# A decoder kernel's first attention phase with another order of its stages, and constants loaded in another order

## The chip, the cores and the metric

The kernel runs as one program on one core of one Trainium2 chip. The metric is device time in microseconds (us) of one execution. All arithmetic is in 32-bit floats.

## The reference

Two decoder layers over x of 4 sequences x 1024 tokens x 256 numbers, with a context of 4 x 77 x 256. Each sublayer is followed by a layer norm of its sum with its input:

```python
x = _layernorm(x + _L0_attn_ref(x, ...))    # retention, 8 heads of 32: chunk by chunk,
#   attn = (q @ k.T) * D;  o = attn @ v + (q * decay_q) @ S
#   S = decay_s * S + (k * decay_k).T @ v
x = _layernorm(x + _L0_xattn_ref(x, ctx_1024, ctx_1024, W_out, b_out))  # softmax(q @ k.T) @ v, 16 heads of 16
x = _layernorm(x + _L0_ffn_ref(x, ...))     # 64 experts, the 8 best of each token, and 2 shared experts
x = _layernorm(x + _L1_attn_ref(x, ...))    # linear attention with a memory of 64 x 64
x = _layernorm(x + _L1_xattn_ref(x, ctx_1024, ...))
x = _layernorm(x + _L1_ffn_ref(x, ...))     # 8 experts, the 2 best of each token
```

## The kernel before

The program has four phases, one after the other on every engine: the first attention (both attention sublayers of layer 0, its router, and the sending of each token's row to the lists of its experts), the first expert phase, the second attention, the second expert phase. `attention_phase` is written once and called for both layers; `first` tells them apart.

An attention phase works in 8 steps of 128 positions of all four sequences (512 tokens). A step passes through some 50 stage parts. The order in which they are issued is a list written out by hand, `SEQUENCE0` for the first attention and `SEQUENCE1` for the second. An entry `(stage, ahead, part)` says: in round n do this part for step n - ahead. `steady` unrolls it over the rounds; entries whose step lies outside 0 to 7 are left out. Every engine walks the same list in program order and does its share of each entry, and semaphores couple the engines. So each engine is a queue: what waits holds up all that stands behind it on that engine.

The stages of the first attention are, in the order of a step's own dependences:

- Retention. `v` and `qk` (q and k) are products 128 x 128 by 512 tokens, moved out by ScalarE and VectorE. `kt` turns k. `ret` are the scores in 32 small products for two sequences, masked by VectorE with `causal`. `mix` forms the output in 64 small products. `up` advances the state. `wo` is the output product, with residual and norm sums on VectorE. `ln1` is the norm's scale on GpSimd and its use on ScalarE.
- Cross attention. `x1t` turns the rows. `mx` are 16 small products for the row maximum, `mt` turns the maxima, `sc` are the scores in 64 small products with the exponential on ScalarE. `pv` are 32 small products and a division on VectorE. `wout` is the output product, `ln2` its norm, `res` the residual with bias.
- Routing. `x2t` turns the rows, `rt` are the router logits, `top` chooses 8 of 64 experts (VectorE), `rank` counts places and yields `slots` (VectorE, L906 to L940). `cwt` and `b2` add the experts' second biases. `put` parts 0 to 7 are four indirect row transfers (scatters) each on GpSimd, from a `z2` buffer into `lists`. Some parts are preceded by a `rest`, a slow operation on four numbers a partition that spaces them out.

`wo`, `wout`, `v`, `qk`, `b2` and `rt` use the whole array in each product ("dense" below). `ret`, `mix`, `mx`, `sc`, `pv` and `up` use 32 rows or 32 columns of it, four side by side ("sparse" below).

PSUM has one wide tile of four banks, used in turn by `ret`, `mx` and `sc`, and four single banks used in rotation by all other product stages. A product waits until its bank was emptied.

SyncE (SP) issues the loads and stores in an order of its own: first `load(0)` (rows of step 0), `load_t(0)` (turned input of step 0), all constants (`loads`), step 1, the expert weights. Then in each of its iterations n it clears a part of `lists` (2 MB each, `lists<-zero`), stores x2s of step n-3, loads rows of step n+1, stores x2t of step n-2, loads turned input of step n+2, and stores the weights and places of step n-2. One semaphore, `consts`, counts all constants, and VectorE, TensorE and GpSimd wait for its full count. Then VectorE prepares `mask2`, `sel`, `scale_qk`, `state_mask`, `keys` and `vals` (L713 to L745, 24 operations counted by `ready`), and TensorE waits for all 24 before its first product (in the second attention, before the first product of step 0; the products of `keys` come ahead).

After the first attention, `with_units` puts 8 units of the shared experts between the last stages, and the expert phase begins with 20 more (L110 inward, L127 outward) before its first group of expert rows (`e_x<-lists`). The rows of step 7 are scattered at the start of the expert phase (L1544).

## Time and profile before

| | |
|---|---|
| time, median of 3 runs (lowest to highest) | 2013.31 us (2005.93 to 2014.84) |
| the profiled execution: its time, its span | 2014.15 us, 2012.2 us |
| busy share of the span: PE, PE weight load, DVE, ACT, POOL | 85%, 67%, 58%, 31%, 44% |
| mean granted clock of TensorE | 0.91 |
| chain that ended last, by engine | PE 60%, DVE 11%, POOL 8%, issue 7%, DMA 5% |
| last `rank` product of the first attention | 603.2 us |
| first expert rows of the first expert phase loaded | from 695.9 us |
| first product of the second attention | 1146.9 us |

PE is TensorE, PEld its weight load, DVE VectorE, ACT ScalarE, POOL GpSimd, SP SyncE. Times within the profile count from the start of the span. In a row of a timeline the columns are start, duration, engine, line of the kernel, operation, output and inputs, and in square brackets how long the engine sat idle before it and what released it. "issue" there means that it waited for nothing that the profile shows. The durations of pipelined products overlap, so a group of them is read from its start to the start of what follows. The granted clock is the share of TensorE's full clock.

### The profile page before, as it was taken

The numbers are of one execution on the slowest core, as the hardware profiler recorded it, in microseconds if no ns is written. First come the engines' busy times: TensorE is split into PE (matmuls) and PEld (weight loads), VectorE is DVE, ScalarE is ACT, GpSimd is POOL, SyncE is SP. The second block draws the span as 40 slices with busy tenths as digits, with TensorE's granted clock in tenths as the row PEclk, the third lists the DMA queues.
The fourth block names the chain that finished last, engine by engine and source line by source line (L and its number), as shares of the span: only waits on it lengthen the run. The fifth ranks groups of instructions, "written<-read, shape, count | busy, mean of one in ns | idle before, by whom it ended". The sixth has DMA issues, their size and how long they took to land.

```text
span 2012.2 us, 45539 instructions
## 1 busy us (share of the span) xinstructions
PE 1711.1 (85%) x17739; PEld 1349.4 (67%) x17739; DVE 1163.6 (58%) x3228; ACT 622.9 (31%) x957; POOL 895.1 (44%) x1000
## 2 busy tenths in 40 slices
PE   3788888888789899998998478899987499999994
PEld 2676666666656566665666345676656499999994
DVE  3576655755532176776656456787765345665554
ACT  0233222332221176544455123354432011111110
POOL 0006557556758201888888856333322201222223
PEclk9999978988679999999999678999887699999997
DMA  9415434545457899987999922113101512333332
GB/s 320 147 36 195 161 133 159 171 145 173 164 171 215 224 289 299 297 271 252 296 299 305 301 78 83 54 65 129 63 33 50 169 49 75 92 95 93 101 92 69
DMA packets 269634, 322.61 MB, mean 160 GB/s; under 512 B 25083, under 2 KB 245487, under 8 KB 268655
## 3 DMA queue, kind: packets, MB, share of 16 engines
q1 hardware_dynamic: 236399, 227.38, 35.7%
q0 software_dynamic: 33024, 92.32, 14.1%
q8 instruction: 144, 2.36, 0.5%
q14 instruction: 67, 0.55, 0.1%
HBM read 157.22 MB, written 162.40 MB: 159 GB/s over the span
## 4 chain that ended last, share of the span: by engine, by line
PE 60%; DVE 11%; POOL 8%; issue 7%; DMA 5%; ACT 3%; another core or an unknown queue 3%; SPq 1%; DVEq 1%; POOLq 0%; ACTq 0%
PE wide L2039 13%; PE d_yp L2051 6%; POOL big L1413 5%; PE wide L1171 4%; PE wide L1174 3%; PE wide L110 3%; PE wide L127 3%; PE bank L1191 3%; PE wide L1158 2%; PE bank L1184 2%; PE bank L1005 2%; PE bank L1148 2%; ACT pt L650 2%; PE bank L1077 2%
## 5 line engine op out<-in xcount | busy, mean ns | idle before, releaser
L1413 POOL DMA_INDIRECT big<-results,slots x256 | 268.4, 1048 | 207.0 <-DMA results<-e_y 127.3
L2039 PE MATMUL wide<-d_xt,d_ws 128*128 128x128 f32 x2272 | 278.4, 276 | 0.6 <-issue 0.6
L2039 PEld LDWEIGHTS wide<-d_xt,d_ws 128*128 128x128 f32 x2272 | 272.1, 193 | 4.5 <-issue 1.0
L588 POOL DMA_INDIRECT lists<-big,slots x160 | 159.1, 994 | 118.5 <-DVE slots L940 72.1
L650 ACT ACTIVATE pt<-wide 77x2048 f32<-77x2048 f32 x64 | 119.9, 1873 | 210.9 <-PE wide L1174 126.7
L1908 POOL DMA_INDIRECT d_picked<-results,slots x64 | 63.8, 997 | 181.5 <-DMA results<-d_y 168.2
L1939 ACT ACTIVATE d_gate<-wide 128x512 f32<-128x512 f32 x71 | 42.4, 597 | 324.6 <-PE wide L2039 320.0
L1428 DVE SCALAR_TENSOR_TENSOR big<-big,weights 128x256 f32<-128x256 f32 x256 | 108.9, 486 | 51.9 <-DMA big<-results,slots 33.9
L2051 PE MATMUL d_yp<-d_wd,d_h 128*128 x568 | 134.2, 379 | 0.0
L110 PE MATMUL wide<-shared_sx,shared_sw 128*128 128x512 f32 x256 | 127.0, 619 | 6.3 <-DMA shared_sx<-res_t 3.8
L127 PEld LDWEIGHTS wide<-shared_sw,shared_sh 128*128 128x128 f32 x512 | 99.8, 196 | 46.3 <-issue 29.9
L545 POOL TENSOR_TENSOR rs<-mv,eps 128x4 f32<-128x4 f32 x32 | 6.5, 202 | 277.1 <-DVE mv L699 276.9
L127 PE MATMUL wide<-shared_sw,shared_sh 128*128 128x256 f32 x512 | 124.9, 388 | 3.6 <-DVE big L1669 3.6
L158 POOL TENSOR_TENSOR rest_ones<-rest_ones 128x4 f32<-128x4 f32 x108 | 118.6, 1098 | 2.1
L2051 PEld LDWEIGHTS d_yp<-d_wd,d_h 128*128 128x128 f32 x568 | 102.6, 190 | 11.0
L1970 DVE COPY d_ws<-big 128x1024 f32 x142 | 92.5, 694 | 27.4 <-issue 26.4
L1559 ACT ACTIVATE e_xt<-e_xp 128x1024 f32<-128x1024 f32 x80 | 82.0, 1025 | 80.6 <-PE e_xp L1688 55.0
L1688 PE MATMUL e_xp<-e_ident,e_x 128*128 128x128 f32 x640 | 86.4, 279 | 21.8 <-DMA e_x<-lists 16.7
L1988 DVE TENSOR_TENSOR d_h<-d_gate,wide 128x512 f32<-128x512 f32 x71 | 48.7, 686 | 97.1 <-PE wide L2039 97.1
L1184 PE MATMUL bank<-pt,vals 77*32 77x128 f32 x2048 | 89.1, 311 | 15.0 <-issue 7.8
L1700 PE MATMUL wide<-e_xt,e_w1s 128*64 128x128 f32 x1280 | 90.2, 284 | 12.0 <-DVE e_w1s L1605 11.8
L1688 PEld LDWEIGHTS e_xp<-e_ident,e_x 128*128 128x128 f32 x640 | 72.1, 142 | 42.1 <-DMA e_x<-lists 26.2
(280 smaller groups left out, 3528.3 us busy)
## 6 DMA issues: line engine op xcount, KB each, us to landing
lists<-zero SPq DMA_DIRECT2D x20, 2048.0 KB, 14.4
e_x<-lists SPq DMA_DIRECT2D x80, 512.0 KB
results<-e_y SPq DMA_DIRECT2D x80, 512.0 KB
d_x<-lists SPq DMA_DIRECT2D x71, 128.0 KB
results<-d_y SPq DMA_DIRECT2D x71, 128.0 KB
e_w<-in_L_w SPq DMA_DIRECT2D x2, 4096.0 KB
x<-in_x SPq DMA_DIRECT2D x8, 512.0 KB
shared_sw<-in_x_t SPq DMA_DIRECT2D x32, 128.0 KB
```

The source lines that it names most:

```text
L110: ins = nc.tensor.matmul(sp_h, self.sw1[:, c, u * P:(u + 1) * P], self.sx[:, s % 2, c], start=c == 0, stop=c == KC - 1)
L127: ins = nc.tensor.matmul(sp_y[b // 2][:, b % 2 * DM:(b % 2 + 1) * DM], self.sh[:, n % 2, b * P:(b + 1) * P], self.sw2[:, u], start=u == 0 ...
L158: step(self.nc.gpsimd.tensor_tensor(self.ones[:, 1], self.ones[:, 0], self.ones[:, 0], ALU.pow))
L588: pool.indirect_dma_start(out=lists, out_offset=bass.IndirectOffsetOnAxis(ap=slots[:, b, i, k:k + 1], axis=0), in_=z2[i % 3][:, b, :], in_ ...
L650: empties(nc.scalar.activation(pt[0:CTX, p % 2].rearrange("k (j n) -> k j n", j=4), ps[0:CTX], ACT.Exp, scale=score_scale), job)
L1184: ins = mm(out[quarter(r), at:at + P], vals[:, p, c * 8 + 2 * r + h], pt[0:CTX, p % 2, of:of + P], start=True, stop=True)
L1413: pool.indirect_dma_start(out=picked[:, c % NG, b, :], out_offset=None, in_=results[0:-(-PAGES_OF_STEP[s] // 4) * 4 * R0, :], in_offset=ba ...
L1428: ins = nc.vector.scalar_tensor_tensor(out=acc[s % NA][:, b], in0=picked[:, n % NG, b], scalar=weights[:, b, s, k:k + 1], in1=acc[s % NA][ ...
L1688: ins = tr(xp[:, h, (a * KC + c) * P:(a * KC + c + 1) * P], x[:, j % NX, h, a, c * P:(c + 1) * P], ident[:])
L1970: nc.vector.tensor_copy(ws[:, T % NW, n], w[:, :, bass.ds(e * H1, H1)]).then_inc(staged, 1)
L2039: ins = mm(out[T % 2][:, a * P:(a + 1) * P], ws[:, T % NW, n, c, a * P:(a + 1) * P], xt[:, T % 2, c], start=c == 0, stop=c == KC - 1)
L2051: ins = mm(yp[T % 2][:, 0:DM], h[:, T % 2, c * P:(c + 1) * P], wd_flat[:, bass.ds(e * (HC * DM) + c * DM, DM)], start=c == 0, stop=c == HC ...
```

## The change

`SEQUENCE0` is another order of the same stage parts. Most of them are one round later or at another place of the round; the sequence now reaches 4 rounds back, and the phase has 12 rounds for 11. Dense and sparse products alternate. `put` parts 0 and 1 stand behind `rank` in the same round (3 back), parts 2 to 7 one round on, with `ln1` between parts 0 and 1 and `ln2` behind part 2.

In the first attention the constants that the retention needs (`soon`, 8 transfers) are issued right behind `load_t(0)` and counted by `consts_soon`. TensorE waits for these alone before its first product, for all constants at the first `wo`, and for `ready` at the first `mx`. VectorE prepares scale and mask of the state first, and the rest (`lay_out`) when it comes to `("mx", 0, 0)`. `ctx_rows` moves to another place of the same buffer.

In the second attention 11 of the 24 constant transfers are issued by ScalarE (`others`), while SP issues the other 13, the context and its two weights first.

```diff
--- before.py
+++ after.py
@@ -206,13 +206,13 @@
 
 
 SEQUENCE0 = [
-    ("wo", 1, 0), ("wo", 1, 1), ("put", 3, 0), ("v", 0, 0), ("v", 0, 1), ("ln1", 1, 0),
-    ("wout", 2, 0), ("wout", 2, 1), ("cwt", 3, 0), ("put", 3, 1), ("qk", 0, 0), ("x1t", 1, 0), ("x1t", 1, 1),
-    ("mx", 1, 0), ("ln2", 2, 0), ("qk", 0, 1), ("b2", 3, 0), ("b2", 3, 1), ("mx", 1, 1), ("res", 1, 0), ("put", 3, 2),
-    ("qk", 0, 2), ("x2t", 2, 0), ("x2t", 2, 1), ("mx", 1, 2), ("put", 3, 3), ("qk", 0, 3), ("mx", 1, 3), ("put", 3, 4),
-    ("kt", 0, 0), ("ret", 0, 0), ("kt", 0, 1), ("put", 3, 5), ("mt", 1, 0), ("rt", 2, 0), ("put", 3, 6), ("put", 3, 7),
-    ("sc", 1, 0), ("mix", 0, 0), ("top", 2, 0), ("ret", 0, 1), ("pv", 1, 0), ("sc", 1, 1), ("mix", 0, 1), ("up", 0, 0),
-    ("rank", 2, 0), ("sc", 1, 2), ("pv", 1, 1), ("sc", 1, 3), ("pv", 1, 2), ("pv", 1, 3),
+    ("wout", 3, 1), ("kt", 1, 0), ("ret", 1, 1), ("mix", 1, 0), ("x1t", 2, 0), ("b2", 4, 0), ("x1t", 2, 1), ("mx", 2, 0),
+    ("put", 4, 2), ("wo", 1, 0), ("kt", 1, 1), ("mx", 2, 1), ("mix", 1, 1), ("ln2", 3, 0), ("put", 4, 3), ("put", 4, 4),
+    ("mx", 2, 2), ("qk", 0, 0), ("b2", 4, 1), ("mx", 2, 3), ("x2t", 3, 0), ("x2t", 3, 1), ("res", 2, 0), ("up", 1, 0),
+    ("mt", 2, 0), ("rt", 3, 0), ("qk", 0, 1), ("put", 4, 5), ("v", 0, 0), ("sc", 2, 0), ("top", 3, 0), ("qk", 0, 2),
+    ("put", 4, 6), ("put", 4, 7), ("rank", 3, 0), ("pv", 2, 0), ("sc", 2, 1), ("cwt", 3, 0), ("put", 3, 0), ("wo", 1, 1),
+    ("pv", 2, 1), ("sc", 2, 2), ("qk", 0, 3), ("sc", 2, 3), ("pv", 2, 2), ("wout", 2, 0), ("pv", 2, 3), ("ret", 0, 0),
+    ("v", 0, 1), ("ln1", 1, 0), ("put", 3, 1),
 ]
 SEQUENCE1 = [
     ("kvt", 1, 0), ("mt", 3, 0), ("wo", 2, 0), ("wo", 2, 1), ("sc", 3, 0), ("ln2", 4, 0), ("num", 1, 0), ("num", 1, 1),
@@ -324,7 +324,7 @@
             prob = spare[:, 0:4096].rearrange("p (h n) -> p h n", h=2)
             z2 = [spare[:, n:n + 1024].rearrange("p (b n) -> p b n", b=NB) for n in (7168, 6144)] + z2
             zero = sb("zero", [P, DM])
-            ctx_rows = prob[0:CTX, 0, 0:NB * DM].rearrange("k (b n) -> k b n", b=NB)
+            ctx_rows = spare[0:CTX, 4096:4096 + NB * DM].rearrange("k (b n) -> k b n", b=NB)
             total = sb("total", [P, NB, 2, RD])
             state = sb("state", [P, NB, 2, 4, RD])
             ot = sb("ot", [P, KC, TS])
@@ -366,6 +366,7 @@
 
         full, free = shared.full, shared.free
         consts = sem("consts")
+        consts_soon = sem("consts_soon") if first else None
         ready = sem("ready")
         pool_ready = sem("pool_ready")
         x_in = [sem(f"x_in{k}") for k in range(2)]
@@ -419,25 +420,31 @@
                 return [(0, at) for at in blanks(0)[n * 2:(n + 1) * 2]]
             return [(n - 2, at) for at in blanks(n - 2)] if n - 2 < STEPS else []
 
-        loads = [(ident[:], d["ident"]), (head_mask[:], d["head_mask"]), (causal[:], d["causal"]),
-                 (wout[:], col(d["wout"])), (bout[:], d["bout"]), (router[:], col(d["router"])),
-                 (before[:], d["before"]), (ones_sq[:], d["ones_sq"]),
-                 (ctx_t, d["ctx_t"].rearrange("b (c p) n -> p b c n", p=P))]
+        loads = [(ident[:], d["ident"]), (head_mask[:], d["head_mask"])]
+        others = [(causal[:], d["causal"]), (wout[:], col(d["wout"])), (bout[:], d["bout"]), (router[:], col(d["router"])),
+                  (before[:], d["before"]), (ones_sq[:], d["ones_sq"])]
+        context = (ctx_t, d["ctx_t"].rearrange("b (c p) n -> p b c n", p=P))
         if first:
-            loads += [(wqk[:, :, 0:DM], col(d["wq"])), (wqk[:, :, DM:], col(d["wk"])), (wv[:], col(d["wv"])),
-                      (wo[:], col(d["wo"])), (scale_qk[:, 0:2], d["decay_q"]), (decay_s[:], d["decay_s"]),
-                      (block_mask[:], d["block_mask"]),
+            loads = [loads[1]] + others[1:] + [context]
+            others = []
+            soon = [(wv[:], col(d["wv"])), (wqk[:, :, 0:DM], col(d["wq"])), (wqk[:, :, DM:], col(d["wk"])),
+                    (scale_qk[:, 0:2], d["decay_q"]), (decay_s[:], d["decay_s"]), (block_mask[:], d["block_mask"]),
+                    (causal[:], d["causal"]), (ident[:], d["ident"])]
+            loads += [(wo[:], col(d["wo"])),
                       (router_b[:], d["router_b"].broadcast_to([P, E])), (b2[:], d["b2"]),
                       (sb2[:], d["sb2"]),
                       (ctx_rows, d["ctx"].rearrange("b k n -> k b n"))]
         else:
+            soon = []
+            loads = [context, (wk[:], col(d["wk"])), (wv[:], col(d["wv"]))] + loads
             loads += [(wlin[:, :, 0], col(d["wq1"])), (wlin[:, :, 1], col(d["wk1"])), (wlin[:, :, 2], col(d["wv1"])),
-                      (wq[:], col(d["wq"])), (wk[:], col(d["wk"])), (wv[:], col(d["wv"])),
-                      (mem_norm[:], d["mem_norm_rows"]), (gate[:], d["gate"]), (iota[:], d["iota"])]
+                      (mem_norm[:], d["mem_norm_rows"])]
+            others = [(gate[:], d["gate"])] + others + [(wq[:], col(d["wq"])), (iota[:], d["iota"])]
             for h in range(2):
                 rows_h = slice(h * MEM, (h + 1) * MEM)
-                loads += [(wo[rows_h], d["wo1"]), (memory[rows_h, 0:MEM], d["memory"]),
-                          (memory[rows_h, MEM:], d["mem_norm"])]
+                others += [(wo[rows_h], d["wo1"])]
+                loads += [(memory[rows_h, 0:MEM], d["memory"]), (memory[rows_h, MEM:], d["mem_norm"])]
+        CONSTS = 16 * (len(loads) + len(others))
         READY = 24 if first else 24
         POOL_READY = 5 if first else 2
 
@@ -462,8 +469,10 @@
                                      src_t[b, :, span].rearrange("(c p) n -> p c n", p=P)).then_inc(xt_in[i % 2], 16)
 
             begin_here(sp)
+            load_t(0)
+            for dst_ap, src_ap in soon:
+                sp.dma_start(dst_ap, src_ap).then_inc(consts_soon, 16)
             load(0)
-            load_t(0)
             for dst_ap, src_ap in loads:
                 sp.dma_start(dst_ap, src_ap).then_inc(consts, 16)
             load(1)
@@ -559,7 +568,7 @@
             if first:
                 nc.gpsimd.memset(zero[:], 0.0).then_inc(pool_ready, 1)
             pool.wait_ge(pool_ready, POOL_READY - (2 if first else 0))
-            pool.wait_ge(consts, 16 * len(loads))
+            pool.wait_ge(consts, CONSTS)
             if first:
                 for n in range(ES):
                     nc.gpsimd.tensor_tensor(b2[:], b2[:], sb2[0:E, n], ALU.add).then_inc(pool_ready, 1)
@@ -606,8 +615,10 @@
                 empties(nc.scalar.activation(out, in_, ACT.Copy), job)
 
             begin_here(act)
+            for dst_ap, src_ap in others:
+                act.dma_start(dst_ap, src_ap).then_inc(consts, 16)
             if not first:
-                act.wait_ge(consts, 16 * len(loads))
+                act.wait_ge(consts, CONSTS)
                 nc.scalar.activation(small[:, 0:1], gate[:], ACT.Exp, scale=-1.0).then_inc(gate_exp, 1)
             for job in order:
                 stage, i, p = job
@@ -709,48 +720,56 @@
                 make(nc.vector.memset(state[:], 0.0))
                 make(nc.vector.memset(v[:], 1.0))
             make(nc.vector.memset(vals[:], 1.0))
-            dve.wait_ge(consts, 16 * len(loads))
-            make(nc.vector.tensor_reduce(mask2[:], ...))
...
             if first:
+                dve.wait_ge(consts_soon, 16 * len(soon))
                 make(nc.vector.reciprocal(scale_qk[:, 2:4], scale_qk[:, 0:2]))
                 make(nc.vector.tensor_scalar(scale_qk[:, 2:4], ...))
                 for g in range(2):
                     make(nc.vector.tensor_scalar(state_mask[:, g]..., block_mask[:], decay_s[:, g:g + 1], ...))
...
+            def lay_out():
+                dve.wait_ge(consts, CONSTS)
+                make(nc.vector.tensor_reduce(mask2[:], ...))
...
+                assert made[0] == READY, made
+
+            if not first:
+                lay_out()
             for job in order:
                 stage, i, p = job
+                if first and job == ("mx", 0, 0):
+                    lay_out()
                 if stage == "late":
                     late_on_vector(dve, i)
                 if stage == "res":
@@ -969,8 +988,10 @@
                 return slice(b * P, (b + 1) * P)
 
             begin_here(pe)
-            pe.wait_ge(consts, 16 * len(loads))
-            if not first:
+            if first:
+                pe.wait_ge(consts_soon, 16 * len(soon))
+            else:
+                pe.wait_ge(consts, CONSTS)
                 for b in range(NB):
                     out = take_bank(("key", b, 0))
                     for g in range(KC):
@@ -980,11 +1001,16 @@
                     for c in range(KC):
                         ins = mm(out[0:CTX, DM:2 * DM], ctx_t[:, b, c], wv[:, c], start=c == 0, stop=c == KC - 1)
                     fills(ins, ("key", b, 0))
-            pe.wait_ge(ready, READY)
             if first:
                 pe.wait_ge(state_done, 1)
+            else:
+                pe.wait_ge(ready, READY)
             for job in order:
                 stage, i, p = job
+                if first and job == ("wo", 0, 0):
+                    pe.wait_ge(consts, CONSTS)
+                if first and job == ("mx", 0, 0):
+                    pe.wait_ge(ready, READY)
                 if stage == "unit":
                     if i == 0:
                         emptied(pe, ("sc", STEPS - 1, NB - 1))
```

## Rows read from the trace of the kernel before

**Rows 1.** Stretches: length, busy PE, PEld, DVE, ACT, POOL, clock, DMA, GB/s.

```profile
27.50:147.90 120.40, 101.76 (x1656) 77.25 (x1656) 63.59 (x115) 32.45 (x45) 4.71 (x12) 0.97 0.43 143
...
106.60:158.30 51.70, 46.13 (x823) 36.61 (x819) 38.84 (x98) 18.19 (x24) 5.12 (x10) 1.00 0.14 42
158.30:225.20 66.90, 56.55 (x833) 42.71 (x830) 41.47 (x104) 18.67 (x25) 40.22 (x47) 0.92 0.50 164
...
433.00:500.20 67.20, 57.44 (x835) 42.61 (x831) 41.37 (x104) 18.63 (x25) 40.45 (x46) 0.92 0.58 191
500.20:571.40 71.20, 54.42 (x538) 42.50 (x534) 34.35 (x98) 15.29 (x19) 47.15 (x52) 0.60 0.62 207
```

**Rows 2.** timeline, all engines, end of the preparation

```profile
18.87 0.16 DVE L713 TENSOR_REDUCE mask<-head_mask 128x2 f32<-128x8 f32 x1 [14.42 <-DMA big<-in_ctx]
...
20.68 1.75 DVE L720 RECIPROCAL scale_qk<-scale_qk 128x256 f32<-128x256 f32 x1
...
23.44 0.64 DVE L743 TENSOR_SCALAR keys<-pt,mask 128x154 f32<-128x154 f32 x2
...
27.49 1.62 PE L1011 MATMUL bank<-wv,shared_sw 128*128 128x256 f32 x3 [27.49 <-DVE vals L745]
```

**Rows 3.** timeline of SP, first transfers issued

```profile
1.22 2.03 SPq L461 DMA_DIRECT2D shared_sw<-in_x_t  x4
...
13.26 0.43 SPq L468 DMA_DIRECT2D big<-in_ctx  x1
```

**Rows 4.** timeline of PE in the round from 365.7 us

```profile
376.63 1.88 PE L1005 MATMUL bank<-shared_sw,wqk 128*128 128x512 f32 x4
...
401.99 0.26 PE L1171 MATMUL wide<-x1t,keys 32*77 32x128 f32 x1 [1.00 <-issue]
...
413.91 0.72 PE L1171 MATMUL wide<-x1t,keys 32*77 32x128 f32 x8 [1.73 <-issue]
```

**Rows 5.** stretches of 10 us in that round

```profile
410.00:420.00 10.00, 7.63 (x118) 5.50 (x114) 4.20 (x6) 0.00 (x0) 7.85 (x8) 0.57 0.26 93
```

**Rows 6.** the page, part 3, DMA queues

```profile
q8 instruction: 144, 2.36, 0.5%
```

**Rows 7.** groups of POOL's instructions in that round

```profile
L588 POOL DMA_INDIRECT lists<-big,slots x33 | 32.9, 998 | 20.3 <-DVE slots L940 11.0 <-issue 7.9 <-POOL rest_ones L158 1.4
L158 POOL TENSOR_TENSOR rest_ones<-rest_ones 128x4 f32<-128x4 f32 x5 | 5.2, 1042 | 0.1
```

**Rows 8.** timeline of DVE, first and last of `rank` in that round

```profile
424.63 0.28 DVE L906 TENSOR_SCALAR pages_i<-bank 128x128 int32<-128x128 f32 x1
...
430.33 0.18 DVE L940 CAST slots<-slot 128x32 uint32<-128x32 f32 x1
```

**Rows 9.** one long stretch of the second attention

```profile
1240.00:1460.00 220.00, 199.92 (x2956) 147.83 (x2955) 173.29 (x553) 93.47 (x141) 81.59 (x101) 0.95 0.22 76
```

**Rows 10.** timeline of PE: first `rank`, last `x1t`, last `wout`, last `rank`

```profile
147.94 0.70 PE L1204 MATMUL bank<-chosen,before 128*128 128x256 f32 x2
...
512.18 0.63 PE L1077 MATMUL bank<-ident,x 128*128 128x128 f32 x4 [2.69 <-ACT x L661]
...
571.43 5.75 PE L1191 MATMUL bank<-wout,att_t 128*128 128x256 f32 x16
...
603.21 0.59 PE L1204 MATMUL bank<-chosen,before 128*128 128x256 f32 x2
```

**Rows 11.** timeline of POOL and of SP, where the first expert phase begins

```profile
667.03 0.96 POOL L1544 DMA_INDIRECT lists<-big,slots  x1 [0.31 <-issue]
...
695.87 1.53 SPq L1476 DMA_DIRECT2D e_x<-lists  x3
```

**Rows 12.** timelines of SP, PE and DVE, start of the second attention

```profile
1142.12 0.60 SPq L468 DMA_DIRECT2D memory<-in_L_norm  x1
...
1146.94 1.96 PE L978 MATMUL bank<-pt,wk 128*128 128x77 f32 x8 [24.01 <-DMA memory<-in_L_norm]
...
1150.72 0.79 DVE L743 TENSOR_SCALAR keys<-bank,mask 128x154 f32<-128x154 f32 x2 [0.90 <-PE bank L981]
```

65 lines of the change are left out of this document (32 added, 33 removed).

## The prediction

> **What bounds the kernel now.** I read the round-by-round stretches first. In the first attention TensorE is busy most of the time, but its speed depends on what else runs. The round from 106.6 us, in which nothing is scattered yet, takes 51.7 us: 46.1 us of products at full clock and 5.6 us of waits. The rounds with scatters have only `cwt` and `b2` more (2.6 us of products), yet the five from 158.3 to 500.2 us take 68.4 us each; their granted clock is 0.92 in the first and the last of them. The next one, with only 538 products, takes 71.2 us at clock 0.60 [rows 1]. So a full round has 46.1 + 2.6 = 48.7 us of products at full clock; without scatters the old order would take 54.3 us, and 14.1 us a round come with the scatters.
>
> The timeline of TensorE shows where. Dense products run undisturbed: four `qk` products take 1.88 us. In the sparse stretch (two `ret`, `sc`, `mix`, `pv`, `up`, 25 us long) it stops again and again, for 1.00 or 1.73 us, with no releaser ("issue") [rows 4], and the clock is 0.57 in 410 to 420 us [rows 5]. When the scatters are over, at 420 us, stops and low clock are gone. Sparse products ask for instructions five times as often as dense ones and more (8 in 0.72 us even at low clock, 4 in 1.88 us [rows 4]), and instructions come by a DMA queue of their own [rows 6], so I take the stops for late instructions behind the scatters' rows. That is a reading; no row names it.
>
> The other engines have room. VectorE is busy 41 us in such a round [rows 1]. GpSimd is busy 40.5 us [rows 1] and has 9.3 us of issue gaps between its scatters and rests (a scatter with its gap is 1.28 us, (32.9 + 7.9 + 1.4) / 33), some 50 us: a floor for the round, 18 us below the present one; it waits 11 us a round for slots [rows 7].
>
> Behind this phase all hangs on TensorE. The last `rank` is at 603.2 us and the first expert rows load at 695.9 us, 92.7 us later, behind 20 units of the shared experts; GpSimd's last scatter starts at 667.0 us, over 25 us earlier [rows 10, 11]. So I follow the `rank` products, eight of them, 147.9 to 603.2 us, and let all that follows shift with the last. Seven intervals, 455.3 us: five full rounds (342) and the last two 113.3 us.
>
> **Part 1, constants of the first attention: the first rank from 147.9 to 132 us.** Before, the constants end at 18.9 us, VectorE prepares for 8.6 us and TensorE starts at 27.5 us [rows 2]. Now SP issues 4 input transfers (2.0 us from 0.7 us) and 8 constants (0.5 us each), done at 7 us. The last constant before landed 5.6 us after its issue with far more bytes ahead of it [rows 2, 3]; I take 3 us: start at 10 us (bounds 8 and 13), 17.5 us sooner. The scale and mask of the state (2.8 us, 20.68 to 23.44 [rows 2]) hide behind the first two `qk`. The rest of the preparation, 8.6 - 2.8 = 5.8 us, now stands on VectorE right behind the second `ret` of round 2, where TensorE has only a `mix` half and `x1t` to do; I count it in full, 5.8 us (bounds 0 and 6). The new order also puts more in front of the first `rank`: of step 3 three `qk` and half a `v`, of step 2 half a `wo`, less one `sc` and one `pv` of step 1: five pieces of 1.75 us less 2.9 us, +5.8 us. Against it stand 19 us in which TensorE idles between 27.5 and 147.9 us (120.4 less its busy time [rows 1]); in the new list the chains `ret`, `mix`, `wo` have other products between them, and I take half back, 10 us (bounds 0 and 19). Sum: 147.9 - 17.5 + 5.8 + 5.8 - 10 = 132, so -16 us (bounds -3 to -32).
>
> **Part 2, the round.** I walked one round of the new list by these durations, each engine in its own order. At full clock and without stops TensorE waits only about 2 us in it. The longest loop through another queue is `rank`, 5.9 us of VectorE up to `slots` [rows 8], four scatters 5.1 us, `ln1` on GpSimd and ScalarE, then `x1t`. From the last `wo` at 500.2 us to its `x1t` at 512.2 us [rows 10] pass 12 us, 5 of them the products, so `ln1` with VectorE's sums is at most 7 us: the loop is 18 us against 17 parts of the list, some 22 of the 48.7 us, that stand between. `pv`, `wout` and `mx` wait behind `rank` on VectorE, and at the round's end they have caught up. SP's order is unchanged; its waits for `b2`, `x1t`, `x2t`, `top` and `rank` move together, half a round later, and `load_t` of step n + 2 still comes half a round before its `qk`. So 48.7 + 2 = 51 us, about GpSimd's floor. What the scatters add decides. If all 14.1 us stay lost on top the round is 65 us; if alternation hides them it is GpSimd's 51 to 52 us. In the new list 64 sparse products have as a rule dense ones on both sides, so instructions are asked for at nearly even pace; but scatters now lie beside the whole round, where they left 17 us of it free. I take 10 us of the 14, nearer to the end at which little is hidden: 61 us (bounds 52 and 68.4, nothing won).
>
> The new intervals: four full rounds (244 us); one without three `qk` and half a `v` (7 us less, 54 us); the last two as before (113.3 us), less 9 of the 12 us from 500.2 to 512.2 us in which the last step's `wo` and `ln1` lay bare before `x1t` [rows 10]: they now run a round sooner beside other work. Sum 402.3 us against 455.3 us: -53 us.
>
> The two levels of the clock are the other lever. TensorE: Matmul & The Clock Gate of the Trainium skill (Why this matters for your kernels) says that the engine falls back when it has long idle gaps between bursts. By that rule 410 to 420 us, with no gap above 1.73 us, would have stayed at full clock; the trace disagrees, and I keep the rows. Runtime: NRT & Kernel Launch of the Trainium skill (Instruction fetch mechanics) says that the fetch is hidden behind the issue of instructions; by that the stops had another cause and alternation would win nothing on them, which is rival 1 below.
>
> **Part 3, constants of the second attention: -3 us.** SP issued 24 constants up to 1142.7 us, 0.58 us each; 11 of them go to ScalarE, idle there, which saves 6.4 us of issue. But VectorE gates it: with its own preparation done it waits only 0.90 us for the first of four `key` products [rows 12]. Four such waits are 3.6 us; I take -3 us, bounds 0 and -6.
>
> **Sum.** 2014.15 us (the profiled execution, 0.8 us above the median of the runs) - 16 - 53 - 3 = 1942 us.
>
> **Rivals.**
> 1. The order wins nothing: the round stays 68.4 us. Then 5 x 68.4 - 7 + 104.3 = 439.3, -16 us; with the heads -35: 1979 us. For it: the same products and scatters, the stops' cause unproven.
> 2. GpSimd becomes the bound: 52 us in five intervals, 364.3, -91 us; in all -110: 1904 us. For it: the walk without stops, which gives TensorE no more than that. Against it: scatters without pause.
> 3. Slower: mixing does not lift the sparse stretches but pulls the dense ones down to the low level, as from 500.2 to 571.4 us, where `wo`, `rt` and `wout` ran at clock 0.60 [rows 1]. At 0.60 the round is 48.7 / 0.60 + 2 = 83 us: 512 us, +57 us, in all +38: 2052 us. It decides above 75.4 us a round ((455.3 + 19 - 97.3) / 5), that is at a mean clock under 0.66. Against it: the second attention, whose list alternates already, holds 0.95 over 220 us at 91% busy, though with less than half the DMA share (0.22) [rows 9].
>
> **How the numbers follow.** The forecast, a round of 56 to 65 us, has 0.50 (1915 to 1965 us); rival 1 with 65 to 72 us 0.22; rival 2 0.16; rival 3 0.10; 0.02 for other losses. Half a per cent, 10 us, is what this kernel's runs can tell. Faster 0.84: all of forecast and rival 2 and nearly all of rival 1; the same 0.05; slower 0.11. The range, 1900 to 1990 us, takes in rival 2's and rival 1's times and leaves out rival 3.
>
> **What the profile would show.** Right: the first product near 10 us; `rank` products first near 132 us and last near 534 us, 61 us apart; granted clock 0.93 or more in the scatter rounds; few stops without releaser in `sc` and `mix`; GpSimd's wait for slots down to 5 to 10 us a round; a pause of some 6 us before the first `mx`; first expert rows near 627 us; the first product of the second attention 5 us sooner within its phase, its first `x0t` only 3 us. Wrong: if the dense products' own durations double in the middle of rounds, or GpSimd waits for slots longer than 11 us.

## The result, and the profile after

The changed kernel takes 2037.7 us (2035.0 to 2045.9, four runs) against 2012.5 us (2005.9 to 2014.8, four runs) for the kernel before: ratio 1.0138, 95% interval 1.0108 to 1.0169. It is slower by 1.4%, where 1942 us, 3.6% less than before, was forecast. The experiments below add something that one measurement can't show: later, the kernel before itself took 1880 to 1885 us, and there the same change is *faster*, ratio 0.9792 (0.977 to 0.9814). I call the two the **long level** (kernel before at 2012 to 2030 us) and the **short level** (1880 to 1885 us). The prediction was made at the long level and is compared with it.

Line numbers of the changed kernel: `rank` 1230, `wout` 1217, `wo` 1091, `qk` 1031, `sc` 1197 and 1200, `pv` 1210, `up` 1084, `rt` 1225, scatter 597, the pause on GpSimd 158, last step's scatters 1570. First the chain that ended last and part of the page, then the stretches between `rank` products (the columns are those of [rows 1]).

```profile
span 2034.1 us, 45537 instructions
...
PE 1743.0 (86%) x17739; PEld 1357.4 (67%) x17739; DVE 1167.1 (57%) x3228; ACT 621.1 (31%) x957; POOL 892.8 (44%) x1000
...
PE 61%; POOL 10%; issue 9%; DVE 7%; DMA 5%; another core or an unknown queue 3%; ACT 3%; SPq 1%; DVEq 1%; POOLq 0%; ACTq 0%
```

```profile
125.32:195.53 70.21, 60.79 (x831) 43.03 (x830) 41.47 (x103) 17.03 (x25) 38.98 (x45) 0.90 0.47 151
195.53:273.05 77.52, 64.73 (x831) 46.63 (x830) 41.81 (x103) 20.32 (x26) 41.33 (x47) 0.87 0.44 144
273.05:348.20 75.15, 64.81 (x831) 46.37 (x830) 41.62 (x103) 18.71 (x26) 40.26 (x45) 0.84 0.44 144
348.20:423.63 75.43, 64.22 (x832) 45.28 (x831) 41.58 (x103) 18.61 (x26) 40.71 (x45) 0.89 0.41 137
423.63:494.00 70.37, 57.06 (x812) 43.46 (x810) 40.41 (x101) 16.45 (x25) 39.31 (x44) 0.83 0.50 162
```

Against [rows 1] the rounds did not shrink from 68.4 to 61 us, they grew to 70.2 to 77.5. In 273.05:348.20 TensorE is busy 64.8 us, where the prediction counted 48.7 at full clock, and idle 10.3. The granted clock of the five rounds is 0.83 to 0.90. The DMA share is no higher than before.

What fills a round is to be seen in the timeline of TensorE (start, length, idle time ahead in brackets), and then in those of SP and GpSimd:

```profile
333.95 3.52 PE L1225 MATMUL bank<-router,x2t 128*128 128x64 f32 x16
337.25 3.73 PE L1031 MATMUL bank<-shared_sw,wqk 128*128 128x512 f32 x4
...
355.61 0.46 PE L1197 MATMUL wide<-x1t,keys 32*77 32x128 f32 x8
...
358.44 0.26 PE L1200 MATMUL wide<-shared_sh,sel 32*77 32x128 f32 x1 [0.27 <-issue]
...
359.87 0.37 PE L1197 MATMUL wide<-x1t,keys 32*77 32x128 f32 x3 [0.45 <-issue]
361.45 0.37 PE L1197 MATMUL wide<-x1t,keys 32*77 32x128 f32 x1 [1.21 <-issue]
...
362.18 3.32 PE L1031 MATMUL bank<-shared_sw,wqk 128*128 128x512 f32 x4
...
369.35 0.46 PE L1197 MATMUL wide<-x1t,keys 32*77 32x128 f32 x4 [0.96 <-issue]
...
372.21 0.71 PE L1200 MATMUL wide<-shared_sh,sel 32*77 32x128 f32 x3 [0.97 <-issue]
```

```profile
355.78 3.95 SPq L486 DMA_DIRECT2D lists<-zero  x2
```

```profile
355.65 0.96 POOL L597 DMA_INDIRECT lists<-big,slots  x1 [10.79 <-DVE slots L959]
```

At 333.95 and 337.25 two dense pieces, `rt` and `qk`, run at about half speed (3.5 and 3.7 us; four `qk` products took 1.88 in [rows 4], and the same 16 `rt` products take 1.9 in a later run without the loss). From 355.6 us one `sc` of 64 products, 1.9 us when undisturbed, takes 6.6 us: stops of 0.26 to 1.21 us without a releaser, one to five products between them. Two things begin there together: GpSimd scatters again, and SP sends the zero fill of 4 MB. I had not placed that fill in the prediction; this was my first suspect (Theory A of the expectations below).

The small terms: the first product starts at 9.56 us (below), the first `rank` at 125.3, and the last at 628.2 instead of 603.2 us [rows 10], so the loss lies between the `rank` products. The first expert rows load 92.1 us after it (92.7 before). In the second attention the first key product comes 17.3 us after the phase's first load instead of 18.6, the first `x0t` 28.4 instead of 29.3.

```profile
9.56 1.22 PE L1031 MATMUL bank<-shared_sw,wqk 128*128 128x512 f32 x1 [9.56 <-DMA ident<-in_ident]
```

### The profile page after: what moved, and what is told of

Its sections match the earlier page's. It is cut to its first block, busy times and chain, and to the rows that moved or that the text cites. A ratio compares the mean times of both kernels' runs of the same rounds, so it can differ in the third digit from the quotient of the medians.

```text
span 2034.1 us, 45537 instructions
## 1 busy us (share of the span) xinstructions
PE 1743.0 (86%) x17739; PEld 1357.4 (67%) x17739; DVE 1167.1 (57%) x3228; ACT 621.1 (31%) x957; POOL 892.8 (44%) x1000
## 3 DMA queue, kind: packets, MB, share of 16 engines
q10 hardware_dynamic: 1840, 1.00, 0.2%
## 4 chain that ended last, share of the span: by engine, by line
PE 61%; POOL 10%; issue 9%; DVE 7%; DMA 5%; another core or an unknown queue 3%; ACT 3%; SPq 1%; DVEq 1%; POOLq 0%; ACTq 0%
PE wide L2065 13%; POOL big L1439 7%; PE d_yp L2077 6%; PE wide L1197 4%; PE wide L1200 4%; PE bank L1210 4%; PE bank L1217 4%; PE bank L1031 3%; PE wide L1184 3%; PE bank L1103 2%; PE bank L1174 2%; PE wide L110 2%; POOL rest_ones L158 2%; PE wide L127 2%
## 5 line engine op out<-in xcount | busy, mean ns | idle before, releaser
L1439 POOL DMA_INDIRECT big<-results,slots x256 | 262.9, 1027 | 209.6 <-DMA results<-e_y 133.0
L158 POOL TENSOR_TENSOR rest_ones<-rest_ones 128x4 f32<-128x4 f32 x108 | 123.4, 1142 | 1.9
L2014 DVE TENSOR_TENSOR d_h<-d_gate,wide 128x512 f32<-128x512 f32 x71 | 48.7, 687 | 96.4 <-PE wide L2065 96.4
L1210 PEld LDWEIGHTS bank<-pt,vals 77*32 77x32 f32 x2048 | 64.0, 123 | 54.1 <-issue 52.6
```

The costliest lines, as they stand in the source:

```text
L158: step(self.nc.gpsimd.tensor_tensor(self.ones[:, 1], self.ones[:, 0], self.ones[:, 0], ALU.pow))
L1210: ins = mm(out[quarter(r), at:at + P], vals[:, p, c * 8 + 2 * r + h], pt[0:CTX, p % 2, of:of + P], start=True, stop=True)
L1439: pool.indirect_dma_start(out=picked[:, c % NG, b, :], out_offset=None, in_=results[0:-(-PAGES_OF_STEP[s] // 4) * 4 * R0, :], in_offset=ba ...
```

## The experiments

Each of the eighteen runs was measured beside the kernel before, on the same chip. Each table row below has the time between successive `rank` products (seven intervals), their sum, and the idle time of TensorE put down to issue within them ("stops"), all added up from the timelines.

```
kernel               level  intervals between rank products, us         sum    stops
before               long   67.0 69.4 71.1 67.3 67.2 55.2 58.1        455.3   32.3
after                long   70.2 77.5 75.1 75.4 70.3 64.9 69.4        502.9   53.0
c2_before_again      short  54.5 54.5 57.1 55.8 54.4 49.4 42.4        368.0    1.2
c1_changed_again     short  51.0 49.7 49.5 51.0 47.7 49.2 52.2        350.3    2.0
e1_head_old_order    short  54.6 54.5 54.5 57.2 55.8 49.0 41.5        366.9    0.8
e2_order_alone       short  51.6 49.7 49.5 50.9 47.7 49.2 52.2        350.8    2.3
e5_new_fill_at_b2    short  49.8 51.1 54.6 50.1 48.8 49.1 52.4        355.7    4.9
e6_old_fill_in_sp.   short  57.8 58.4 58.0 58.1 58.2 49.6 42.4        382.5   10.2
e7_new_fill_first    short  88.1 49.6 49.7 49.5 47.7 49.1 52.2        385.8    3.5
e8_old_fill_first    short  61.1 57.6 54.5 54.4 54.5 51.5 42.6        376.1    3.2
f3_new_double_fill   long   75.5 75.3 75.0 73.7 75.4 61.0 72.8        508.7   58.3
f4_old_double_fill   long   71.0 71.1 71.3 71.1 71.5 56.8 56.9        469.7   31.2
g1_new_no_rest       long   88.0 88.5 88.8 88.7 87.1 85.1 85.2        611.4  114.5
g2_old_no_rest       long   78.9 78.6 78.6 78.5 78.7 74.2 73.6        541.1   87.1
h1_new_more_rest     short  50.2 58.7 62.6 63.0 64.2 61.6 62.3        422.6    0.4
h3_new_no_scatter    short  50.1 49.5 49.5 49.7 47.4 50.5 51.9        348.6    0.9
h4_old_no_scatter    short  54.0 55.4 54.0 54.0 55.6 48.4 39.7        361.2    0.6
h6_head_again        short  57.7 54.5 54.5 54.4 57.1 50.6 41.8        370.5    0.0
h7_new_mixed         long   50.0 49.5 70.3 77.8 56.9 56.6 63.1        424.1   20.3
h8_new_even_rest     short  50.3 49.5 52.1 54.6 53.2 52.2 56.6        368.3    0.6
```

### The two parts apart: e1, e2

e1 is the changed kernel with `SEQUENCE0` of before; e2 is the kernel before with the new `SEQUENCE0`, no other line.

> The changed kernel with the order of the first attention put back to what it was before: the sooner constants, the deeper preparation and the three sooner rows of scatters stay only where they belong to the loads, the written order is the old one. If the loss sits in the rounds, as the trace after reads (head 22.6 us sooner, then 47.6 us lost in seven rounds), this kernel keeps the head's gain and loses nothing: first rank product near 132, rank intervals near 65 us, total about 1990 to 1998 us (ratio 0.989 to 0.993). If the loss came with the loads or the moved preparation (a transfer of constants on ScalarE's queue that is late, a slower engine order), it would stay slower than before: above 2015 us.

> The kernel before with the new order alone; constants and preparation as before. If the order carries the loss, its rank intervals sum to about 500 us instead of 455 and the total is about 2050 to 2060 us (ratio 1.019 to 1.024), more than the changed kernel, since the gain at the head is missing. If the loss came from the loads, it is at or below the time before (1960 to 2015 us).

Measured: e1 0.9943 (0.9928 to 0.9958), e2 0.983 (0.9799 to 0.986), beside a kernel before of 1881 us. The head gained nearly what was expected (its first `rank` comes at 137.6 us instead of near 132), the order did the opposite: its intervals sum to 350.8 us and not to 500. Both runs fell on the short level, and neither part was ever run alone at the long one; that the loss there is the order's is read from the trace, where all of it lies between the `rank` products. Before any mechanism could be discussed, the change itself had to be measured at the short level.

### The whole change and the kernel before again: c1, c2

> The changed kernel once more, unaltered, beside the kernel before. On the chip of the last four runs the kernel before took 1881 us and not 2012, and the order alone was 1.7% faster there and not slower. If the sign of the change depends on the chip, this run on that chip gives a ratio of 0.975 to 0.99 (1835 to 1862 us); if the new loads spoil what the order wins, it is above 1 again (over 1885 us).

> The kernel before, unaltered, for its profile on this chip. If it is the same chip as that of the last four runs: about 1881 us, with rank intervals near 61 us and few stops put down to issue, a granted clock near 0.94; the 130 us beneath the first measurement then sit in stretches where the first profile shows stops and a low clock. If the 130 us lie evenly over all stages instead, the chip is faster in everything.

Measured: 1840.7 us, ratio 0.9792 (0.977 to 0.9814); the kernel before again 1885.6 us. Two stretches between `rank` products of c1, then one of c2, and what GpSimd waits for in one round of each:

```profile
227.52:277.02 49.50, 49.23 (x831) 37.74 (x830) 41.48 (x103) 18.61 (x26) 39.67 (x45) 1.00 0.67 215
277.02:328.01 50.99, 49.73 (x832) 37.92 (x831) 41.42 (x103) 18.61 (x26) 40.88 (x46) 1.00 0.63 206
```

```profile
POOL lists L597 <- issue: 8.4, 28, 0.3
POOL lists L597 <- POOL rest_ones L158: 1.4, 5, 0.3
```

```profile
151.81:206.29 54.48, 48.63 (x836) 38.52 (x831) 41.81 (x103) 19.04 (x26) 34.19 (x40) 1.00 0.57 185
```

```profile
POOL lists L588 <- issue: 7.3, 25, 0.3
POOL rs L545 <- DVE mv L699: 4.3, 1, 4.3
POOL lists L588 <- DVE slots L940: 4.1, 1, 4.1
...
```

In c1 TensorE is busy 49.2 of 49.5 us at clock 1.00 and GpSimd waits for no other engine. In c2 the old order leaves TensorE idle for some 6 us a round, 54.5 us; the long level's [rows 1] have 68.4 for the same products. The same pieces that took 6.6 us (from 355.61) and 7.4 us (from 365.43) in the trace of the changed kernel above are clean in c1, although the zero fill and scatters run beside them there as well (timelines of TensorE, SP and GpSimd):

```profile
284.42 0.46 PE L1197 MATMUL wide<-x1t,keys 32*77 32x128 f32 x8
...
286.34 1.98 PE L1031 MATMUL bank<-shared_sw,wqk 128*128 128x512 f32 x4
288.40 0.46 PE L1197 MATMUL wide<-x1t,keys 32*77 32x128 f32 x8
...
290.32 1.08 PE L1210 MATMUL bank<-pt,vals 77*32 77x128 f32 x32
```

```profile
284.69 3.74 SPq L486 DMA_DIRECT2D lists<-zero  x2
```

```profile
285.87 0.96 POOL L597 DMA_INDIRECT lists<-z,slots  x1 [0.30 <-issue]
```

The two levels are not two kinds of chip: chip 9 ran the kernel before in 1884 us at one time and in 2016 us later. Behind the last `rank` product the level costs both kernels the same: the rest of the span is 1409.0 and 1405.9 us (before and changed) at the long level, 1363.2 and 1358.7 at the short one. So the sign turns between the `rank` products: 455.3 against 502.9 us, then 368.0 against 350.3.

### The place of the zero fill: e5, e6, e7, e8

```diff
-                for k, at in clearing(n):
-                    sp.dma_start(lists[at * CLEAR * R0:(at + 1) * CLEAR * R0, :].rearrange("(p t) n -> p t n", p=P),
-                                 zero[:].unsqueeze(1).broadcast_to([P, CLEAR * R0 // P, DM])).then_inc(blank[k], 16)
                 if n == 1:
                     sp.dma_start(units.sb1[:], d["sb1"]).then_inc(units.sb1_in, 16)
                 if 0 <= n - 3 < STEPS:
...
+                for k, at in clearing(n):
...
```

That is e5, with the fill behind the store of `x2s`; e6 puts it behind `load_t(n + 2)` in the kernel before. e7 and e8 change only `clearing`, so that round 2 returns all later pieces at once.

> The changed kernel with one thing moved: the zero fill of 4 MB a round is issued by SP behind the store of x2 rows (some 25 us earlier in a round, beside dense products) and no longer behind the scatter places, where the new order has its sparse score products. Theory A (full DMA engines starve the many short instructions of sparse products): the stretch sc(2), sc(3), pv loses its 10 us of stops, a part of it comes back where the fill now falls; 5 to 8 us a round less, total 1985 to 2005 us. Theory B (the low clock on dense products, the fill has no part): total within 6 us of the changed kernel, 2030 to 2045 us. Theory C (the fill hurts anything beside it): moved loss, 2025 to 2045 us, with the stops now at L1084, L1184 and rt.

> The kernel before with its zero fill issued behind the loads of the next columns, in the middle of the round, so that it falls beside the old order's sparse stretch (mix, ret, sc) and no longer beside wo, v and wout. Theory A (full DMA engines starve short instructions): 5 to 8 us a round more, total 2050 to 2065 us. Theory B or C: within 10 us of before.

> The changed kernel with all zero fills of the steps behind the first issued in round 2, some 40 MB at once, so that rounds 5 to 10 hold no fill. Rounds 2 to 4 are spoilt by it (the queue of SP is held for about 120 us), so only the later rank intervals count. Theory A (fill beside sparse products): later intervals 6 to 10 us below those of the changed kernel on the same chip. Theory B (low clock on dense products): within 2 us of them.

> The kernel before with the same early fill. Theory A: the fill lay beside dense products there and cost little, so its later rank intervals fall by at most 3 us. Theory C (the fill costs wherever it lies): by 6 us or more too.

Measured: e5 0.9811 (0.9773 to 0.9849), not to be told from c1 by its time, though its intervals sum to 5 us more; e6 1.0102 (1.007 to 1.0133), with rounds of 58 us instead of 55 and 10.2 us of stops instead of 1.2; e7's later rounds are c1's, e8's are c2's. These four ran at the short level, so they don't decide what the fill does at the long one. They show that the fill beside the old order's sparse stretch does make stops (e6), and that in the new order it costs little where it stands: the rounds of e7 without it are at most 1.5 us shorter than c1's.

### More fill, fewer pauses: f3, f4, g1, g2

f3 and f4 send each fill a second time, to a tensor nobody reads. g1 and g2 drop the pause ahead of four scatters:

```diff
-                    elif part_no > 2 or i >= STEPS - 2:
-                        shared.rest(pool)
```

> The changed kernel with each zero fill written twice, the second time to a tensor that nothing reads: 8 MB a round in place of 4, 25 us a round in which all 16 DMA engines are full. Theory A (full DMA engines starve TensorE of instructions in sparse products): stops put down to issue grow from 2 us to 10 us or more over the seven rounds, and the round grows by 3 us or more, here more than in the kernel before, as the new order has sparse products everywhere. Theory D (the stops of the first measurement have nothing to do with transfers but with that chip's supply of instructions): stops stay under 4 us, the round within 1.5 us of 49.6, as long as no transfer that is needed comes late.

> The kernel before with the same doubled fill, which now reaches from the dense block into the next products. Theory A: stops grow too, but less than in the new order (3 to 8 us over seven rounds); Theory D: under 3 us. Under both the round may grow where the x and x_t loads queue behind 25 us of fill.

> The changed kernel without the pauses on GpSimd ahead of the scatters of the first attention (a 1.03 us power operation on a tile of ones, five a round and sixteen in the last two steps; the result does not use them). On the chip of the last four runs the round of the new order was 49.6 us and GpSimd waited in it for no one, so GpSimd set it. If so, the round falls by about 5 us, to 44 to 46 us, and the total by 30 to 40 us beneath the changed kernel's 1841 (ratio to before 0.958 to 0.964). If TensorE set the round, nothing changes (0.976 to 0.981). If this runs where the first measurement ran (the kernel before takes 2012 us, stops of TensorE), GpSimd waits there anyway for slots, and the gain is under 5 us.

> The kernel before without the same pauses. In its round of 54.5 us GpSimd waited 8.4 us for the slots and for the sums of ln2, so TensorE's chain sets it: rank intervals stay within 1 us of 54.5 and the total within 10 us of before (ratio 0.995 to 1.0). If GpSimd set this round too, 30 us less, as for the new order.

These ran at the long level (kernel before 2030 us). Twice the fill: 2052 and 2038 us in one run each. The traces with one fill are those of `after` and `before`, taken at another time, when the kernel before took 2012 us: against them the mean of the first five intervals is 1.3 us longer (new) and 2.8 us longer (old), the stops are 58 against 53 us and 31 against 32. Twice the fill does not make twice the stops; as the main cause (Theory A) it falls for the long level. Less pause: 1.0604 (1.0575 to 1.0634) and 1.0366 (1.0336 to 1.0397). I had expected nothing or a gain for both; both lost heavily. A round of g2, in three stretches: scatters in groups of four with other work of GpSimd between them, then 22 scatters with nothing between them, then none. The last line is the part of the second stretch in which TensorE stops. Behind them some of TensorE's rows there, and a scatter.

```profile
384.83:416.00 31.17, 28.77 (x350) 22.20 (x343) 24.27 (x67) 10.71 (x16) 13.46 (x19) 1.00 0.55 181
416.00:447.00 31.00, 12.92 (x98) 8.67 (x97) 5.64 (x6) 1.68 (x3) 21.23 (x22) 0.61 0.44 147
447.00:463.33 16.33, 14.04 (x392) 12.71 (x391) 11.37 (x31) 6.30 (x7) 0.00 (x0) 0.80 0.04 10
430.00:447.00 17.00, 5.01 (x16) 3.53 (x15) 0.00 (x0) 0.00 (x0) 10.53 (x11) 0.50 0.26 94
```

```profile
437.36 0.27 PE L1197 MATMUL bank<-router,x2t 128*128 128x64 f32 x1 [0.92 <-issue]
438.76 0.27 PE L1197 MATMUL bank<-router,x2t 128*128 128x64 f32 x1 [1.13 <-issue]
```

```profile
438.87 0.96 POOL L586 DMA_INDIRECT lists<-big,slots  x1 [0.30 <-issue]
```

In the second stretch TensorE runs 98 products in 31 us and is idle for 18: it waits 6.1 us for VectorE up to 428 us, and from 430 us on, when 14 scatters have followed each other every 1.26 us, it stops 14 times, 11.7 us in all. From there it gets 16 products in 17 us, often one each 1.40 us, and these are `router` products and other dense ones. Behind the last scatter 392 products run in 16.3 us. GpSimd's own scatters keep their 1.26 us nearly throughout. Here the suspect changes: it is the scatters, and how closely they follow each other (Theory S).

### With more pauses and without scatters: h1, h3, h4, h6

h1 puts a pause ahead of each two scatters; in h3 and h4 a power operation stands in for every scatter of steps 0 to 6; h6 is e1's kernel.

```diff
+                    if part_no <= 2 and i < STEPS - 2:
+                        shared.rest(pool)
                     for k in range(at, at + 4):
+                        if k == at + 2:
+                            shared.rest(pool)
                         pool.indirect_dma_start(
```

> The changed kernel with more pauses between GpSimd's scatters: one ahead of each two scatters in place of one ahead of each four from the fourth row on (16 a round of 1.03 us in place of 5). Where the kernel before takes 2012 to 2030 us, theory S (scatters that follow each other closely starve TensorE of instructions) expects stops put down to issue under 15 us over the seven rounds in place of 54, a round of 64 to 68 us in place of 72, and a ratio of 0.96 to 0.99. Where the kernel before takes 1881 us there are no stops to win, GpSimd sets the round, and the eleven pauses more cost 11 to 13 us a round: ratio 1.02 to 1.04. If the stops have another source, this is slower on either chip.

> The changed kernel in which the scatters of the first attention's steps 0 to 6 are left out: each is replaced by a power operation of about the same time on GpSimd, so the lists hold zeros where rows would be. On a chip where the kernel before takes 2012 to 2030 us, theory S expects no stops put down to issue at all (under 3 us) and a round of 46 to 52 us with everything else, the zero fill too, in place. If the stops come from the transfers of SP or from the order of the products alone, most of the 54 us stay. On a chip of 1881 us: a round of 46 to 50 us.

> The kernel before with the same scatters left out in the same way. Theory S: no stops, a round of 53 to 55 us on either chip. The difference to the run before it is then what the order wins by itself on TensorE's chain: 4 to 8 us a round.

> The head of the change with the old order, once more. On a chip of 1881 us it was 0.9943. If this run is on a chip where the kernel before takes 2012 to 2030 us, the loads help there too and nothing else moves: 0.986 to 0.993, against 1.014 for the whole change, so the whole of the loss is the order's.

These fell on the short level (1884 us). h1 1.0181 (1.0132 to 1.023): GpSimd, which waits there for no other engine, sets intervals of 62 to 64 us from the third on. In h3 and h4 the lists hold zeros in place of the rows. h3 and h4, one run each, 1840 and 1867 us, with most rounds at 49.5 and 54.0 us: at the short level scatters cost TensorE next to nothing, and the order is worth 4.5 us a round by itself. h6 0.9926 (0.9904 to 0.9948), as e1.

### Three kinds of rounds in one run: h7

As the level can't be chosen, the comparison was put inside one run. In step i of the scatters' loop:

```diff
+                        if i in (4, 5) and (k == at + 2 or k == at and part_no <= 2):
+                            shared.rest(pool)
+                        if i < 2:
...
+                            nc.gpsimd.tensor_tensor(ones[:, 1], ones[:, 0], ones[:, 0], ALU.pow).then_inc(idled, 1)
...
+                        else:
                             pool.indirect_dma_start(
```

> The changed kernel with three kinds of rounds in one run, so that they are compared on one chip: for steps 0 and 1 the scatters are left out (power operations of about the same time stand in, so the lists hold zeros for these rows), steps 2 and 3 scatter as in the changed kernel, steps 4 and 5 with a pause ahead of each two scatters, step 6 as before. All rows of a step are scattered between its rank product and the next. Theory S on a chip where the kernel before takes 2012 to 2030 us: intervals 1 and 2 at 48 to 53 us without stops, 3 and 4 at 72 to 77 us with 7 us or more of stops each, 5 and 6 at 62 to 67 us with under 3 us of stops. If the stops come with the order and the transfers of SP alone, intervals 1 and 2 are 68 to 75 us like the others. On a chip of 1881 us: 49.5, 49.5, 49.5, 50, 62, 62 us, with no stops anywhere.

It ran at the long level (kernel before 2016 us). The seven stretches between its `rank` products, and what TensorE waits for in the second, the fourth and the fifth:

```profile
126.36:176.30 49.94, 49.55 (x831) 38.07 (x830) 41.28 (x103) 18.61 (x26) 38.36 (x43) 1.00 0.42 134
176.30:225.80 49.50, 49.23 (x832) 37.71 (x831) 41.32 (x103) 18.66 (x26) 42.52 (x47) 1.00 0.43 135
225.80:296.10 70.30, 60.48 (x831) 44.06 (x830) 41.63 (x103) 17.03 (x25) 42.78 (x49) 0.85 0.46 149
296.10:373.90 77.80, 64.60 (x831) 46.52 (x830) 41.73 (x103) 20.32 (x26) 41.70 (x47) 0.87 0.42 138
373.90:430.80 56.90, 46.41 (x812) 36.48 (x810) 40.29 (x101) 18.32 (x25) 41.66 (x46) 0.97 0.55 179
430.80:487.40 56.60, 43.04 (x527) 33.94 (x527) 31.45 (x88) 15.52 (x19) 47.37 (x53) 0.75 0.60 195
487.40:550.50 63.10, 49.50 (x431) 35.53 (x432) 22.71 (x78) 16.84 (x19) 46.37 (x49) 0.77 0.48 161
```

```profile
PE wide L1194 <- DVE shared_sh L862: 0.2, 1, 0.2
...
PE bank L1220 <- ACT pt L671: 3.6, 1, 3.6
PE wide L1207 <- issue: 3.3, 6, 1.0
...
PE bank L1094 <- issue: 1.7, 4, 0.5
PE wide L1210 <- issue: 1.6, 5, 0.5
...
PE bank L1082 <- issue: 1.2, 4, 0.3
PE bank L1094 <- issue: 1.0, 2, 0.5
```

Without scatters the new round is 49.5 us at clock 1.00, without one stop, at the long level too, and with the zero fills in place. With the usual scatters it is 70.3 and 77.8 us, with 4.0 and 7.0 us of stops and the clock at 0.85 and 0.87 (72 to 77 us and 7 us or more of stops each were expected). With 16 pauses instead of 5 the two intervals are 56.9 and 56.6 us with 2.1 and 1.1 us of stops, 5 us below what was expected. The 56.9 us are no price of a steady round: the scatters of step 4 with their pauses take GpSimd from 382.5 to 443.7 us, 61 us, so it falls behind, and part of its work is done in the last interval, 63.1 us. The expectation's sentence that all rows of a step are scattered before the next `rank` does not hold for these two steps. The last three intervals together take 176.6 us against 204.6 in the changed kernel.

### A smaller step of spacing: h8

h8 is the changed kernel with a pause ahead of every four scatters, the first three rows too (8 instead of 5 a round).

> The changed kernel with a pause ahead of every four scatters in the first three rows of a step too (8 a round in place of 5), so that no twelve scatters follow each other without one; the output is the whole one. Where the kernel before takes about 1880 us: GpSimd sets the round and gets 3 us more, 52.5 to 53.5 us in place of 49.6, ratio 0.988 to 0.995. Where it takes 2012 to 2030 us, theory S: a third to a half of the stops gone, rounds of 64 to 70 us in place of 72, ratio 0.975 to 1.0, so that one spacing is at least no loss under both conditions. If it is the count of scatters and not their spacing that makes the stops, the ratio stays at 1.014 or above there.

It fell on the short level: 0.9858 (0.9827 to 0.9889), two rounds of 50 us and then three of 52.1 to 54.6 us, about the price expected. What it does at the long level was not measured, nor h1 as a whole there. So no kernel that does all the work was seen to beat the kernel before at the long level; at the short one no kernel that does it was measured faster than the changed one.

## Why the prediction was wrong, point by point

**The step that failed** is in Part 2: "In the new list 64 sparse products have as a rule dense ones on both sides, so instructions are asked for at nearly even pace ... I take 10 us of the 14 ...: 61 us (bounds 52 and 68.4, nothing won)". The scatters' surcharge on a round was carried over from the old order as if alternation could only shrink it. It differs from order to order: 68.4 - 54.0 (h4) = 14.4 us in the old, and in the new 74.6 (mean of the first four intervals) - 49.5 (h3, h7) = 25.1 us. One of the prediction's own signs of being wrong came true with it, the dense products at twice their duration in the middle of a round. (h4 ran at the short level; the old order without scatters was not run at the long one, and the round from 106.6 us, from which the prediction has its 14.1 us, had no zero fill beside it either, with a DMA share of 0.14 [rows 1].) Even the upper bound left out a loss. The same sentence's other half, that scatters "now lie beside the whole round, where they left 17 us of it free", had the reason for it and was given no price. In the old order the dense block lay in the free time and ran at full clock [rows 4]; in the new one dense products are drawn into the low clock as well (`rt` 3.5 us, `qk` 3.7, above), of the 25 us some 14 are longer busy time and 11 are waits, 8 of them stops. The clock makes at most 9 of the 14 (an estimate: 1 - 0.875, the mean clock of the four rounds, of 74.6 us); the rest goes with products that run singly and count 0.26 us each, where eight in a row take 0.46. How much comes from the alternation and how much from the rows of scatters moved a round sooner was not tried apart.

**The reading of the cause was right about the scatters, and its mechanism is not borne out.** "I take the stops for late instructions behind the scatters' rows": at the long level there are none without scatters (h7), with closer ones they multiply (g1, g2), and with wider ones they fade (h7). My own first reading of the trace after, the zero fill, was wrong: right place and time, but doubling it adds little. That *instructions* come late by their queue [rows 6] does not fit. The queue moves the same 144 packets at either level, with 0.5% of the engines' time. From 436 to 454 us of g2, in which TensorE stops nine times, this is all that the DMA engines move:

```profile
DMA packets 338, 0.92 MB, mean 51 GB/s; under 512 B 113, under 2 KB 113, under 8 KB 338
...
q0 software_dynamic: 338, 0.92, 14.3%
```

It is GpSimd's queue alone: no packet of an instruction queue, and none of the zero fill. From 358 to 370.5 us of the changed kernel, with eight stops, the queue of [rows 6] moves nothing either. So these stops are no wait for instructions that this queue had still to bring, and they need no fill. And they fell on dense products, which by the prediction ask for few instructions. Single products at 0.70 or 1.40 us look like something that holds up each instruction; what it is stays open.

Runtime: NRT & Kernel Launch of the Trainium skill (Instruction fetch mechanics) says that the fetch is hidden behind the issue of instructions. By that rule the stops have another cause than the fetch, and the two stretches without a packet of the queue, with nine and eight stops, agree. The prediction drew from it that alternation would win nothing on them, which is so at the long level (32.3 us of stops in seven intervals before, 53.0 after).

**The walk was right within 1.5 us.** 48.7 us of products and 2 of waits gave 51 us without stops; h3 and h7 have 49.5. The 54.3 us worked out for the old order without scatters is h4's 54.0.

**Part 1**: -16 forecast, -22.6 measured at the long level, -25 at the short one (151.8 to 126.8). The loads alone bring the first `rank` to 137.6 us (e1), the order alone to 136.7 (e2), both together to 126.8. So the loads are worth 14.2 us, where -17.5 + 5.8 = -11.7 was forecast, and the order on top of them 10.8 us, where it was +5.8 for more pieces and -10 for filled waits, together -4.2. Which of the order's two terms was off was not measured apart.

**The last two intervals**: forecast "as before ... less 9", 104.3 us. Measured 134.3. At the short level the new order has 101.4 against 91.8 there, so it gives back 10 us with no stops at all, and the "less 9" had the wrong sign at either level; in c1's last interval TensorE waits 4.2 us for `counts` and 2.9 for `att_t`.

```profile
PE bank L1230 <- DVE counts L901: 4.2, 1, 4.2
PE bank L1217 <- DVE att_t L869: 2.9, 1, 2.9
```

**Part 3**: -3 forecast, -1 measured. SP issues its 13 transfers in 9.3 us, 0.72 us each where 24 took 0.58 each, and TensorE still waits for the last of them (`memory<-in_L_norm`).

**The rivals.** Rival 3 named the sign, and its 2052 us is near; but its mechanism is only part of it, for the clock is 0.83 to 0.90 and not 0.60, stops increase too, and its first five rounds, 73.7 us in the mean, stay under its own bound of 75.4 us: the last two intervals decide. Rival 2's round of 52 us is nearly what happens at the short level; removing GpSimd's pauses, which it would have suggested, is the worst edit of all at the long one. Rival 1 happened nowhere.

In one sum: head -22.6, rounds +47.6, second attention -1 make +24.0; the profiled executions differ by 2037.1 - 2014.2 = 22.9 us.

## What to carry to other kernels

A surcharge that is measured in one order of work belongs to that order: carry over what causes it (here how many scatters run beside how many products) and price it again. Leave the possibility open that it grows. Where GpSimd issues many scatters, the gaps between them are part of the schedule. Removing them at the long level cost 3.7% in the old order and by the ratios to the kernel before some 4.6% in the new (1.0604 / 1.0138), and a burst of them is the first thing to look at when TensorE stops without a releaser. Take the time of the kernel before each time you measure: the same pair of kernels came out at 1.014 and at 0.979, and a change whose sign hangs on this needs both told.

## What the runs showed of the hardware that I had not expected

- The kernel before has two levels of time on one core, 1880 to 1885 and 2012 to 2030 us, also on the same chip (chip 9) at different times. What sets the level is open. At the long level TensorE stops beside GpSimd's scatters (70 to 78 us a round with them, 49.5 without); at the short level 32 scatters a round cost it nothing (49.5 us with and without). A scatter takes GpSimd 1.26 us at either level.
- At the long level, under scatters without a pause (g2, 430 to 447 us), TensorE gets about one product each 0.70 or 1.40 us, products of 64 columns as those of 128, while the scatters keep their own 1.26 us. No packet of an instruction queue moves from 436 to 454 us, with nine stops in it.
- With a second zero fill of 4 MB a round the first five intervals were 1.3 and 2.8 us longer in the mean, against traces of another time at the same level.
